# An LSTM cell update as one 24-number scan on VectorE, in place of two dependent instructions

## The chip, the cores and the metric

The kernel runs on one core of a Trainium2 chip, in one launch. The metric is the device time of that launch in microseconds (us); lower is better. TensorE (PE) multiplies matrices, ScalarE (ACT) applies functions, VectorE (DVE) does elementwise work, GpSimd (POOL) fills constants here, SyncE (SP) issues transfers. Each engine takes its instructions in order; engines tell one another by semaphores that something is done.

## The reference

The input x is 4 sequences of 256 steps of 128 numbers. A conditioned attention block and a causal attention give `x + attention`; then an LSTM runs over the 256 steps, a feed-forward block is applied to its outputs, and the result is added to x. Cut to the part that the change touches:

```python
def step(carry, xw_t):                       # 256 times, each on the one before
    prev_h, prev_c = carry                   # 4 x 128
    a = xw_t + prev_h @ Wh                   # 4 x 512
    i = sigmoid(a[:, :H]);       f = sigmoid(a[:, H:2*H])
    o = sigmoid(a[:, 2*H:3*H]);  g = tanh(a[:, 3*H:])
    next_c = f * prev_c + i * g
    next_h = o * tanh(next_c)
    return (next_h, next_c), next_h
x = x + attention(...)
x = x + ffn(lstm(x, h0=cond))                # ffn: gelu(h @ w1 + b1) @ w2 + b2
```

## The kernel before

The program has two stretches. Up to 155 us come the loads, the first block of attention and the feed-forward part that belongs to it. Then a loop over the 256 LSTM steps runs, and everything else that is left (the causal attention in chunks of 32 steps, the second half of the first block, the last feed-forward block) is slipped between the steps.

One step takes four engines in turn. The hidden size of 128 lies on the partitions, so a gate is 128 x 4 numbers (4 sequences), and the four gates are 16 numbers per partition.

- PE (L1738) adds the product with the last h to the gates in the accumulator: 12 small matmuls, four with `wha`, four with `whb`, four with the low part of h. The first eight wait for the high part of h, the last four for its low part.
- ACT (L809) takes the tanh of all 16 numbers into `gates`. Sigmoids are had from tanh, sigmoid(z) = (1 + tanh(z/2)) / 2; the halves are folded into the weights. The gates lie in the order o, i, f, g, and behind them, in the same tile, the old cell (doubled).
- DVE (L1355) forms `pr`, one product for i and g and one for f and the old cell, in one instruction on 8 numbers; then (L1356) the factor from o; then (L1358), which waits for `pr`, adds the two products to the new cell.
- ACT (L811) takes the tanh of the new cell into `h_fac`.
- DVE (L1362) multiplies it with the factor from o: the high part of h, in f16, which PE waits for. L1364, a scan over 12 numbers per partition, leaves what f16 lost as the low part.

The order of all other work is written out by hand. `PLAN` says for each chunk of the attention at which step each of its pieces stands, and `attend(c, t)` issues them on each engine. `VEC_GAP`, `VEC_REST`, `ACT_REST` and `PE_REST` say how many pieces of the first block's second half stand in a step; on DVE a piece of `VEC_GAP` stands between the cell and the wait for its tanh, `attend` and `VEC_REST` stand behind L1364. `INPUTS_AT` and `FFN_STEPS` place the next chunk's gate inputs and the last feed-forward block. An instruction that waits holds up all that stands behind it on its engine.

Before the loop, GpSimd makes `whb` (L552) and fills two constant columns of the tile for h (L555, L556), which the tile names `vaug` in the trace.

Of the kernel before, what the change touches and what calls it, by code (L numbers as in the profile page):

```python
# [23 lines left out]
ALU = mybir.AluOpType  # L24
# [10 lines left out]
P = 128  # L35
# [53 lines left out]
H_SCALE = 4096.0  # L89
W_SCALE = 16.0  # L90
A_SCALE = H_SCALE * W_SCALE
BF16_PARTS = 3
BIAS_ROWS = BF16_PARTS * 4
VW = HD + 1
# [2 lines left out]
def adaln_attention_lstm_ffn(nc, x, cond, w_q, b_q, w_k, b_k, w_v, b_v, w_o, b_o, w_f1, b_f1, w_f2, b_f2,  # L97
                             w_ada, b_ada, W_dq, W_uq, W_dkv, W_uk, W_uv, W_o, Wx, Wh, b_g, w1, b1, w2, b2, out):
    with ExitStack() as ctx:
        def sb(name, shape, dt=F32):  # L100
            return ctx.enter_context(nc.sbuf_tensor(name, shape, dt))
# [4 lines left out]
        def sem(name):  # L106
            return ctx.enter_context(nc.semaphore(name))
# [94 lines left out]
        mo = sb("mo", [P, H, HD])  # L202
        bg_parts = p_mla[0:1].rearrange("p a n -> p (a n)").bitcast(BF16)[:, 0:BIAS_ROWS * D].rearrange("p (r n) -> p r n", n=D)

        gates = sb("gates", [P, 2, 5 * B])
        pr = sb("pr", [P, 2, 2 * B])
        h_fac = sb("h_fac", [P, 2, B, 3])
        h0 = sb("h0", [P, B])
        h_parts = vaug[:].rearrange("p t h v -> p (t h v)").bitcast(F16)[:, 0:2 * S * B * 3].rearrange("p (a t b s) -> p a t b s", a=2, t=S, b=B)
# [108 lines left out]
        w1_ready = sem("w1_ready")  # L318
        gates_mm = sem("gates_mm")
        gates_act = sem("gates_act")  # L320
        c_new = sem("c_new")
        th_act = sem("th_act")
        p_ready = sem("p_ready")
        ff_mm = sem("ff_mm")
        gel_ready = sem("gel_ready")
        y_mm = sem("y_mm")
# [127 lines left out]
        @block.sync  # L454
        def _(sp):
            sp.dma_start(cond4[:], cond).then_inc(ld_ada, 16)
            sp.dma_start(ada_w[:], w_ada).then_inc(ld_ada, 16)
            sp.dma_start(wqkv[:, 0, :], w_q).then_inc(ld_qkv, 16)
            sp.dma_start(wqkv[:, 1, :], w_k).then_inc(ld_qkv, 16)
            sp.dma_start(wqkv[:, 2, :], w_v).then_inc(ld_qkv, 16)  # L460
            sp.dma_start(bqkv[:, 0, :], spread(b_q)).then_inc(ld_qkv, 16)
            sp.dma_start(bqkv[:, 1, :], spread(b_k)).then_inc(ld_qkv, 16)
            sp.dma_start(bqkv[:, 2, :], spread(b_v)).then_inc(ld_qkv, 16)

            sp.dma_start(wd[:, 0, :], W_dq).then_inc(ld_mla, 16)
            sp.dma_start(wd[:, 1, :], W_dkv).then_inc(ld_mla, 16)
            sp.dma_start(wu[0:32, 0, :], W_uq).then_inc(ld_mla, 16)
            sp.dma_start(wu[32:64, 0, :], W_uk).then_inc(ld_mla, 16)
            sp.dma_start(wu[32:64, 1, :], W_uv).then_inc(ld_mla, 16)
            sp.dma_start(wo_m[:], W_o).then_inc(ld_mla, 16)  # L470


            for w_s, w_d, ld in ((wx, Wx, ld_wx), (wh, Wh, ld_rnn)):
                src = w_d.rearrange("k (g n) -> k g n", g=4)
                sp.dma_start(w_s[:, 0, :], src[:, 2, :]).then_inc(ld, 16)
                sp.dma_start(w_s[:, 1:3, :], src[:, 0:2, :]).then_inc(ld, 16)
                sp.dma_start(w_s[:, 3, :], src[:, 3, :]).then_inc(ld, 16)
                if ld is ld_wx:
                    for bb in range(B):
                        sp.dma_start(x_tb[bb:P:B, :, :], x_steps[bb]).then_inc(ld_xtb, 16)  # L480
                    bsrc = row(b_g).rearrange("a (g n) -> a g n", g=4)
                    sp.dma_start(bg[:, 0, :], bsrc[:, 2, :]).then_inc(ld_wx, 16)
                    sp.dma_start(bg[:, 1:3, :], bsrc[:, 0:2, :]).then_inc(ld_wx, 16)
                    sp.dma_start(bg[:, 3, :], bsrc[:, 3, :]).then_inc(ld_wx, 16)
            sp.dma_start(wo_c[:], w_o).then_inc(ld_cff, 16)
            sp.dma_start(bo_c[:], spread(b_o)).then_inc(ld_cff, 16)
            sp.dma_start(wf1[:], w_f1).then_inc(ld_cff, 16)
            sp.dma_start(bf1[:], column(b_f1, FC), allow_slow_non_contiguous=True).then_inc(ld_cff, 16)
            sp.dma_start(wf2[:], w_f2.rearrange("(c p) d -> p c d", p=P)).then_inc(ld_cff, 16)
            sp.dma_start(bf2[:], spread(b_f2)).then_inc(ld_cff, 16)  # L490
            sp.dma_start(w1s[:], w1).then_inc(ld_rnn, 16)
            sp.dma_start(b1s[:], column(b1, FC), allow_slow_non_contiguous=True).then_inc(ld_rnn, 16)
            sp.dma_start(w2s[:], w2.rearrange("(c p) d -> p c d", p=P)).then_inc(ld_rnn, 16)
            sp.dma_start(b2s[:], row(b2)).then_inc(ld_rnn, 16)

            sp.wait_ge(adaR_ready, 1)
            sp.dma_start(bf1_rows, spread(b_f1)).then_inc(ld_bf1, 16)
            sp.wait_ge(bias_part, 2 * BF16_PARTS - 1)
            sp.dma_start(bg_rows[:], bg_parts).then_inc(bias_ready, 16)

            for p, (c, a, z) in enumerate(PIECES):
                sp.wait_ge(y_ready, p + 1)
                sp.dma_start(out_steps[c, a // B:z // B], o_sb[a:z, c % 2, :]).then_inc(stored[c % 2], 16)
            for k in range(2):
                sp.wait_ge(stored[k], 16 * sum(c % 2 == k for c, _, _ in PIECES))

        @block.gpsimd
        def _(pool):
# [29 lines left out]
                                        pattern=[[0, STEPS], [-1, 4], [0, B]], channel_multiplier=1).then_inc(masks, 1)  # L538
                pool.wait_ge(masks, 13 + i)

            pool.wait_ge(w_ready, 4)
            bias = bg[:].rearrange("a g n -> a (g n)")
            for i in range(BF16_PARTS):
                part = bg_parts[:, 4 * i:4 * i + 4, :].rearrange("a g n -> a (g n)")
# [3 lines left out]
                    nc.gpsimd.tensor_tensor(bias, bias, part, ALU.subtract).then_inc(bias_part, 1)  # L548
                    pool.wait_ge(bias_part, 2 * i + 2)

            pool.wait_ge(w_ready, 7)
            nc.gpsimd.tensor_tensor(whb[:], wh[:], wha[:], ALU.subtract).then_inc(w_ready, 1)  # L552

            pool.wait_ge(pv_mm, len(UNITS) // 2)
            nc.gpsimd.memset(h_off[:, :, :, 0], -1.0).then_inc(h_consts, 1)  # L555
            nc.gpsimd.memset(h_off[:, :, :, 1], 0.0).then_inc(h_consts, 1)  # L556
            pool.wait_ge(w1_ready, 1)
# [5 lines left out]
        def _(act):  # L563
# [44 lines left out]
            act.wait_ge(w_mla_mm, 1)  # L608
            nc.scalar.activation(w_mla[:, 0, :], bank[:, 4, 0:D], ACT.Copy).then_inc(w_mla_ready, 1)
            nc.scalar.activation(w_mla[:, 1:3, :].rearrange("p a n -> p (a n)"), bank[:, 5, D:3 * D], ACT.Copy).then_inc(w_mla_ready, 1)  # L610
            act.wait_ge(ld_wx, 16 * 6)
            for w in (wx, bg):
                for g0, g1, f in ((0, 3, .5), (3, 4, 1.)):
                    nc.scalar.mul(w[:, g0:g1, :], w[:, g0:g1, :], A_SCALE * f).then_inc(w_ready, 1)

            nc.scalar.preload_act_table_set(TANH_EXP)
# [117 lines left out]
            o_copy(3)  # L734
            until(first, "up")
            until(first, "third")
            act.wait_ge(ld_rnn, 16 * 7)
            for g0, g1, f in ((0, 3, .5), (3, 4, 1.)):
                nc.scalar.mul(wh[:, g0:g1, :], wh[:, g0:g1, :], W_SCALE * f).then_inc(w_ready, 1)
            act.wait_ge(w_ready, 6)  # L740
            nc.scalar.activation(flat(wha[:]), flat(wh[:]), ACT.Copy).then_inc(w_ready, 1)
            nc.scalar.mul(h0[:], condT[:], H_SCALE).then_inc(w_ready, 1)
            until(first, "fourth")
# [58 lines left out]
            for t in range(S):  # L802
                k = t % 2
                src = bank[:, 6 + (t // STEPS) % 2, (t % STEPS) * GW:(t % STEPS + 1) * GW]

                if t == 0:
                    act.wait_ge(c_new, 1)
                act.wait_ge(gates_mm, t + 1)
                nc.scalar.activation(gates[:, k, 0:GW], src, ACT.Tanh, scale=1.0 / A_SCALE).then_inc(gates_act, 1)  # L809
                act.wait_ge(c_new, t + 2)  # L810
                nc.scalar.activation(h_fac[:, k, :, 1], gates[:, 1 - k, 4 * B:5 * B], ACT.Tanh, scale=0.5).then_inc(th_act, 1)  # L811
                for c in attending(t):
                    attend(c, t)
                go_on(second, ACT_REST, t)
                for p, i in feeding(t):
                    if i in (2, 3):
                        gelu(p, range(2 * i - 4, 2 * i - 2))
# [3 lines left out]
        def _(vec):  # L821
# [11 lines left out]
            def step(ins, signal=None):  # L833
                done(go(ins, signal))
# [492 lines left out]
                    done(mr_ready)  # L1327
                    V.tensor_tensor(mo[:], tr[:, :, 0:HD], rdm[:].unsqueeze(2).to_broadcast([P, H, HD]), ALU.mult).then_inc(mo_normed, 1)

            step(V.memset(gates[:], 0.0), c_new)  # L1330
            vec.wait_ge(h_consts, 2)
            attend(0, PLAN[0]["vb"][0])
            for q in range(2):
# [17 lines left out]

            for t in range(S):
                k = t % 2
                vec.wait_ge(gates_act, t + 1)
                V.scalar_tensor_tensor(pr[:, k, :], gates[:, k, B:3 * B], 1.0, gates[:, k, 3 * B:5 * B], ALU.add, ALU.mult).then_inc(p_ready, 1)  # L1355
                V.tensor_scalar(h_fac[:, k, :, 2], gates[:, k, 0:B], 1.0, 0.5 * H_SCALE, ALU.add, ALU.mult)  # L1356
                vec.wait_ge(p_ready, t + 1)
                V.scalar_tensor_tensor(gates[:, 1 - k, 4 * B:5 * B], pr[:, k, B:2 * B], 0.5, pr[:, k, 0:B], ALU.mult, ALU.add).then_inc(c_new, 1)  # L1358
                go_on(second, VEC_GAP, t)

                vec.wait_ge(th_act, t + 1)
                V.tensor_tensor(h_off[:, t, :, 2], h_fac[:, k, :, 2], h_fac[:, k, :, 1], ALU.mult).then_inc(h_ready, 1)  # L1362
                vec.wait_ge(h_ready, t + 1)
# [1 line left out]
                                     h_off[:, t].rearrange("p b s -> p (b s)"), 0.0, ALU.mult, ALU.subtract).then_inc(hb_ready, 1)  # L1365
                for c in attending(t):
                    attend(c, t)
                go_on(second, VEC_REST, t)
                for p, i in feeding(t):
                    if i == 6:  # L1370
# [4 lines left out]
        def _(pe):  # L1375
# [34 lines left out]
            for k in range(2):  # L1410
                for t in range(4):
                    ins = T.transpose(bank[:, k, t * P:(t + 1) * P], x_tb[:, 4 * k + t, :], ident[:])
                ins.then_inc(x_turned, 1)
            pe.wait_ge(w_ready, 2)
            pe.wait_ge(woT_ready, 1)
            T.matmul(bank[:, 6, :], woT[:], wx[:].rearrange("p g n -> p (g n)"), start=True, stop=True).then_inc(wox_mm, 1)

# [261 lines left out]
            pe.wait_ge(masks, 15)  # L1679
            inputs_of(0, range(0, 5))  # L1680
            pe.wait_ge(vbd_ones, 1)
            pe.wait_ge(w_ready, 9)
            for g in range(4):
                T.matmul(bank[:, 6, g * B:(g + 1) * B], wh[:, g, :], h0[:], start=False, stop=True, skip_group_check=True)

# [99 lines left out]
```

## Time and profile before

| | |
|---|---|
| time, median of 3 runs | 580.17 us (579.87 to 582.31) |
| profiled execution: span from first to last instruction | 578.5 us; about 1.7 us of the run's time lie around it |
| busy: PE, PE weight loads, DVE, ACT, POOL | 412.2, 311.5, 370.7, 241.9, 25.8 us |
| loop of 256 steps, first to last gate tanh | 155.3 to 571.7 us |
| TensorE clock granted in the loop | about half of full speed |

The profile is of one execution. Times in rows are us from the start of the span, unless a column says ns. Of a busy share one cannot read what a stage waits for; the chain of work that ended last, and the rows of one step, show it.

### The profile page before, as it was taken

The page shows a single profiled execution, that of the slowest core. Times are in us where ns is not written, and L with a number is a line of the kernel's source. Part 1 is how long each engine was busy: PE and PEld are TensorE (multiplying, and loading weights), DVE is VectorE, ACT ScalarE, POOL GpSimd, SP SyncE. Part 2 cuts the span into 40 slices and gives each one's busy share as a digit, 9 for nine tenths or more (in the row PEclk, how much of TensorE's full clock was granted, in tenths as well). Part 3 has the DMA queues.
Part 4 walks back from the last instruction along what each step waited for, and adds up shares of the span by engine and source line. Part 5 has one row for each costly group of instructions (what it writes and reads, how often), then busy time and mean ns, then how long its engine had stood idle before and what let it go on. Part 6 is the DMA issues. An engine that isn't in the chain of part 4 may idle for free.

```text
span 578.5 us, 15950 instructions
## 1 busy us (share of the span) xinstructions
PE 412.2 (71%) x6273; PEld 311.5 (54%) x6273; DVE 370.7 (64%) x1967; ACT 241.9 (42%) x937; POOL 25.8 (4%) x35
## 2 busy tenths in 40 slices
PE   3464866676776798995478686886885675787876
PEld 2234644455555575874356554654653564575654
DVE  7888448369687776567756656666667664444443
ACT  1267966363435345234334424334424334333332
POOL 8012000003100000000000000000000000000000
PEclk9676987595555555575555555555555555555555
DMA  7400000000000000000000000000000000000000
GB/s 190 116 0 1 4 2 1 1 1 1 1 2 3 2 3 1 2 2 2 2 3 2 3 1 1 3 2 2 2 3 1 3 2 2 6 11 6 6 11 6
DMA packets 8966, 5.95 MB, mean 10 GB/s; under 512 B 2004, under 2 KB 8252, under 8 KB 8892
## 3 DMA queue, kind: packets, MB, share of 16 engines
q1 hardware_dynamic: 7708, 4.03, 2.8%
q8 instruction: 49, 0.80, 0.6%
q10 hardware_dynamic: 1184, 0.92, 0.5%
q14 instruction: 25, 0.20, 0.1%
HBM read 4.42 MB, written 0.52 MB: 9 GB/s over the span
## 4 chain that ended last, share of the span: by engine, by line
PE 37%; DVE 36%; ACT 18%; issue 7%; DMA 1%; ACTq 0%; DVEq 0%
PE bank L1738 17%; ACT h_fac L811 7%; DVE vaug L1362 6%; ACT gates L809 6%; DVE pr L1355 6%; DVE gates L1358 5%; PE bank L1563 4%; DVE h_fac L1356 3%; PE bank L1640 2%; PE bank L1465 2%; DVE mx L1293 1%; ACT p_mla L756 1%; PE bank L1538 1%; PE bank L1530 1%; PE bank L1512 1%
## 5 line engine op out<-in xcount | busy, mean ns | idle before, releaser
L1738 PE MATMUL bank<-vaug,wha 128*128 128x4 f16 x2040 | 123.8, 169 | 100.0 <-DVE vaug L1362 94.8
L1738 PEld LDWEIGHTS bank<-vaug,wha 128*128 128x128 f16 x2040 | 96.4, 106 | 162.1 <-DVE vaug L1362 160.0
L809 ACT ACTIVATE gates<-bank 128x16 f32<-128x16 f32 x256 | 47.2, 184 | 146.5 <-PE bank L1738 144.6
L811 ACT ACTIVATE h_fac<-gates 128x4 f32<-128x4 f32 x256 | 53.1, 207 | 110.7 <-DVE gates L1358 110.7
L1355 DVE SCALAR_TENSOR_TENSOR pr<-gates 128x8 f32<-128x8 f32 x256 | 42.7, 167 | 77.8 <-ACT gates L809 73.6
L1362 DVE TENSOR_TENSOR vaug<-h_fac 128x4 f16<-128x4 f32 x256 | 43.3, 169 | 67.8 <-ACT h_fac L811 67.6
L1738 PE MATMUL bank<-vaug,whb 128*128 128x4 f16 x1020 | 62.7, 166 | 0.0
L1364 DVE TENSOR_TENSOR_SCAN vaug<-h_fac,vaug 128x12 f16<-128x12 f32 x256 | 46.7, 183 | 8.7
L1563 PE MATMUL bank<-kT,qz 32*128 32x32 f32 (+7 forms) x256 | 50.1, 520 | 0.8 <-ACT kT L775 0.4
L1738 PEld LDWEIGHTS bank<-vaug,whb 128*128 128x128 f16 x1020 | 46.7, 103 | 0.0
L1356 DVE TENSOR_SCALAR h_fac<-gates 128x4 f32<-128x4 f32 x256 | 41.5, 162 | 0.0
L1358 DVE SCALAR_TENSOR_TENSOR gates<-pr 128x4 f32<-128x4 f32 x256 | 41.5, 162 | 0.0
L756 ACT ACTIVATE p_mla<-bank,mx 128x32 f32<-128x32 f32 (+7 forms) x128 | 39.6, 374 | 1.9 <-DVE mx L1293 1.8
L1303 DVE STREAM_TRANSPOSE pt_mla<-p_mla 128x192 f32<-128x192 f32 (+5 forms) x96 | 32.8, 356 | 1.3 <-PE bank L1585 0.6
L1563 PEld LDWEIGHTS bank<-kT,qz 32*128 32x128 f32 x256 | 29.4, 305 | 2.6 <-ACT kT L775 0.8
L1585 PE MATMUL bank<-vbd,pt_mla 128*32 128x36 f32 x1152 | 27.8, 257 | 2.9 <-DVE pt_mla L1303 1.2
L1293 DVE TENSOR_REDUCE mx<-bank 128x2 f32<-128x320 f32 (+7 forms) x48 | 25.6, 539 | 1.9 <-PE bank L1568 1.9
L1585 PEld LDWEIGHTS bank<-vbd,pt_mla 128*32 128x32 f32 x1152 | 21.0, 157 | 5.3 <-DVE pt_mla L1303 4.3
L1444 PE MATMUL bank<-qS,kS 32*128 32x128 f16 x256 | 11.4, 237 | 15.4 <-ACT q_sq L636 7.7
L1636 PE MATMUL bank<-x_tm,wx 128*128 128x128 f32 x64 | 21.5, 472 | 0.0
L1727 PE MATMUL bank<-w2s,ta 128*128 128x128 f32 (+2 forms) x72 | 21.0, 451 | 0.4 <-ACT ta L799 0.4
L1444 PEld LDWEIGHTS bank<-qS,kS 32*128 32x128 f16 x256 | 6.6, 100 | 20.8 <-ACT q_sq L636 9.9
(292 smaller groups left out, 680.4 us busy)
## 6 DMA issues: line engine op xcount, KB each, us to landing
x_tm<-in_x ACTq DMA_DIRECT2D x1, 512.0 KB, 5.3
x_tb<-in_x SPq DMA_DIRECT2D x4, 128.0 KB, 2.7
wf<-in_L_cond_w_f SPq DMA_DIRECT2D x2, 256.0 KB, 3.4
out_y<-tb SPq DMA_DIRECT2D x7, 64.0 KB, 2.0
ada_w<-in_L_cond_w_ada SPq DMA_DIRECT2D x1, 384.0 KB
ada_b<-in_L_cond_b_ada ACTq DMA_DIRECT2D x1, 384.0 KB, 5.8
w1s<-in_L_ffn_w SPq DMA_DIRECT2D x1, 256.0 KB
w2s<-in_L_ffn_w SPq DMA_DIRECT2D x1, 256.0 KB
```

The lines of the kernel that those rows point to most:

```text
L756: ins = nc.scalar.activation(p_mla[:, m % 2, i * n:(i + 1) * n], bank[:, at, i * n:(i + 1) * n], ACT.Exp, bias=mx[:, m % 2, i:i + 1])
L809: nc.scalar.activation(gates[:, k, 0:GW], src, ACT.Tanh, scale=1.0 / A_SCALE).then_inc(gates_act, 1)
L811: nc.scalar.activation(h_fac[:, k, :, 1], gates[:, 1 - k, 4 * B:5 * B], ACT.Tanh, scale=0.5).then_inc(th_act, 1)
L1303: V.transpose(pt_mla[:, to, n * part:n * (part + 1)], p_mla[:, m % 2, n * part:n * (part + 1)]).then_inc(mt_ready, 1)
L1355: V.scalar_tensor_tensor(pr[:, k, :], gates[:, k, B:3 * B], 1.0, gates[:, k, 3 * B:5 * B], ALU.add, ALU.mult).then_inc(p_ready, 1)
L1356: V.tensor_scalar(h_fac[:, k, :, 2], gates[:, k, 0:B], 1.0, 0.5 * H_SCALE, ALU.add, ALU.mult)
L1358: V.scalar_tensor_tensor(gates[:, 1 - k, 4 * B:5 * B], pr[:, k, B:2 * B], 0.5, pr[:, k, 0:B], ALU.mult, ALU.add).then_inc(c_new, 1)
L1362: V.tensor_tensor(h_off[:, t, :, 2], h_fac[:, k, :, 2], h_fac[:, k, :, 1], ALU.mult).then_inc(h_ready, 1)
L1364: V.tensor_tensor_scan(h_low[:, t].rearrange("p b s -> p (b s)"), h_fac[:, k].rearrange("p b s -> p (b s)"), h_off[:, t].rearrange("p b s ...
L1563: T.matmul(bank[:, at, i * n:(i + 1) * n], qz[rows, c % 2, bs[i]].rearrange("p j t -> p (j t)"), kT[rows, bs[i], 0:n], start=(i == 0), sto ...
L1585: ins = T.matmul(bank[32 * b:32 * b + 32, 5, g * GROUP * VW:(g + 1) * GROUP * VW], pt_mla[:, place, i * n + kb * STEPS:i * n + (kb + 1) * ...
L1738: ins = T.matmul(acc[:, g * B:(g + 1) * B], w[:, g, :], h, start=False, stop=True, skip_group_check=True)
```

## The change

The cell update becomes one `tensor_tensor_scan` (op: state = in0 x state + in1) over 6 numbers for each of the 4 sequences, 24 per partition. With s a fixed scale, t_i and t_f the tanh values of the halved gates, g the tanh of the fourth, and c the old cell times s, the six states of one sequence are: s; t_i s + s; that times g; that divided by c, plus t_f; half of that plus a half; that times c. The last is s times the new cell. The quotient needs 1/c, which a new `reciprocal` makes after each step, and a c that is never zero, which a new bitwise or on the cell's bits sees to (it sets one bit of the exponent, which every cell above 2^-63 has set anyway).

So the gates move: ACT writes them to strided places among the scan's two inputs and into a third piece. `wx`, `wh` and the bias are kept in the order f, g, i, o, loaded with two transfers each in place of three and scaled by three instructions in place of two. Constants of the scan's inputs are filled by seven new memsets on GpSimd. The tiles reuse older ones: `hn` holds the scan's inputs (and o), `small` the scan's output.

```diff
-        gates = sb("gates", [P, 2, 5 * B])
-        pr = sb("pr", [P, 2, 2 * B])
+        gates = hn[:].rearrange("p a t h -> p (a t h)")[:, 0:6 * B * CW].rearrange("p (k a b s) -> p k a b s", k=2, a=3, b=B)
+        cell_out = small[:, 0:2 * CW * B // TILES, :].rearrange("p k t -> p (k t)").rearrange("p (k b s) -> p k b s", k=2, b=B)
+        cell_in1, cell_in0, gate_o = gates[:, :, 0], gates[:, :, 1], gates[:, :, 2, :, 0]
+        gates_out = [bass.AP(hn, 3 * k * B * CW + 3, [[3 * TILES * H, P], [(B - 1) * CW + 4, 2], [B * CW - 1, 2], [CW, B]]) for k in range(2)]
...
             pool.wait_ge(pv_mm, len(UNITS) // 2)
+            nc.gpsimd.memset(cell_in1[:, :, :, 0:2], C_SCALE).then_inc(cell_consts, 1)
+            nc.gpsimd.memset(cell_in1[:, :, :, 2:6:3], 0.0).then_inc(cell_consts, 1)
...
             nc.gpsimd.memset(h_off[:, :, :, 0], -1.0).then_inc(h_consts, 1)
...
-                nc.scalar.activation(gates[:, k, 0:GW], src, ACT.Tanh, scale=1.0 / A_SCALE).then_inc(gates_act, 1)
-                act.wait_ge(c_new, t + 2)
-                nc.scalar.activation(h_fac[:, k, :, 1], gates[:, 1 - k, 4 * B:5 * B], ACT.Tanh, scale=0.5).then_inc(th_act, 1)
+                nc.scalar.activation(gates_out[k], src.rearrange("p (u v b) -> p u v b", u=2, v=2), ACT.Tanh, scale=1.0 / A_SCALE).then_inc(gates_act, 1)
+                act.wait_ge(c_new, t + 1)
+                nc.scalar.activation(h_fac[:, k, :, 1], cell_out[:, k, :, 5], ACT.Tanh, scale=1.0 / C_SCALE).then_inc(th_act, 1)
...
                 k = t % 2
+                if t:
+                    vec.wait_ge(c_inverse, t)
                 vec.wait_ge(gates_act, t + 1)
-                V.scalar_tensor_tensor(pr[:, k, :], gates[:, k, B:3 * B], 1.0, gates[:, k, 3 * B:5 * B], ALU.add, ALU.mult).then_inc(p_ready, 1)
-                V.tensor_scalar(h_fac[:, k, :, 2], gates[:, k, 0:B], 1.0, 0.5 * H_SCALE, ALU.add, ALU.mult)
-                vec.wait_ge(p_ready, t + 1)
-                V.scalar_tensor_tensor(gates[:, 1 - k, 4 * B:5 * B], pr[:, k, B:2 * B], 0.5, pr[:, k, 0:B], ALU.mult, ALU.add).then_inc(c_new, 1)
+                V.tensor_tensor_scan(cell_out[:, k].rearrange("p b s -> p (b s)"), cell_in0[:, k].rearrange("p b s -> p (b s)"),
+                                     cell_in1[:, k].rearrange("p b s -> p (b s)"), 0.0, ALU.mult, ALU.add).then_inc(c_new, 1)
+                V.tensor_scalar(h_fac[:, k, :, 2], gate_o[:, k], 1.0, 0.5 * H_SCALE, ALU.add, ALU.mult).then_inc(o_ready, 1)
                 go_on(second, VEC_GAP, t)
+                if t < S - 1:
+                    vec.wait_ge(c_new, t + 1)
+                    V.tensor_scalar(cell_in0[:, 1 - k, :, 5].bitcast(I32), cell_out[:, k, :, 5].bitcast(I32), C_LEAST_BITS, None,
+                                    ALU.bitwise_or).then_inc(c_kept, 1)
+                vec.wait_ge(o_ready, t + 1)
                 vec.wait_ge(th_act, t + 1)
                 V.tensor_tensor(h_off[:, t, :, 2], h_fac[:, k, :, 2], h_fac[:, k, :, 1], ALU.mult).then_inc(h_ready, 1)
...
                 for c in attending(t):
                     attend(c, t)
+                if t < S - 1:
+                    vec.wait_ge(c_kept, t + 1)
+                    V.reciprocal(cell_in0[:, 1 - k, :, 3], cell_in0[:, 1 - k, :, 5]).then_inc(c_inverse, 1)
                 go_on(second, VEC_REST, t)
```

On DVE, a step of the loop in which a row maximum of the attention (`mx`) stands is before, from one gate instruction to the next (the list names a scan SCALAR_TENSOR_TENSOR, and the tile of h `vaug`):

```order
L1355 SCALAR_TENSOR_TENSOR pr<-gates 128x8 [waits gates_act]
L1356 TENSOR_SCALAR h_fac<-gates 128x4
L1358 SCALAR_TENSOR_TENSOR gates<-pr 128x4 [waits p_ready]
L1362 TENSOR_TENSOR vaug<-h_fac 128x4 [waits th_act]
L1364 SCALAR_TENSOR_TENSOR vaug<-h_fac,vaug 128x12 [waits h_ready]
L1293 TENSOR_REDUCE mx<-bank 128x2 [waits mp_ready,ms_mm]
```

The same step in the changed kernel, whose lines are numbered 10 to 24 higher, has the scan into `small`, and the or and the reciprocal on pieces of `hn`:

```order
L1369 SCALAR_TENSOR_TENSOR small<-hn 128x24 [waits gates_act,c_inverse]
L1371 TENSOR_SCALAR h_fac<-hn 128x4
L1375 TENSOR_SCALAR hn<-small 128x4 [waits c_new]
L1380 TENSOR_TENSOR vaug<-h_fac 128x4 [waits th_act,o_ready]
L1382 SCALAR_TENSOR_TENSOR vaug<-h_fac,vaug 128x12 [waits h_ready]
L1305 TENSOR_REDUCE mx<-bank 128x2 [waits mp_ready,ms_mm]
L1388 RECIPROCAL hn<-hn 128x4 [waits c_kept]
```

Two instructions ahead of the cell's tanh became one, the or stands between the cell and the wait for its tanh, and the reciprocal stands behind the attention's piece and ahead of the next step's scan, which now waits for it too.

On GpSimd, the end of the stretch before the loop, from the last piece of the bias on, is before:

```order
L545 CAST p_mla<-bg 1x512 [waits bias_part]
L552 TENSOR_TENSOR whb<-wh,wha 128x512 [waits w_ready,bias_part]
L555 MEMSET vaug 128x1024 [waits pv_mm]
L556 MEMSET vaug 128x1024
L558 CAST ada_w<-w1s 128x512 [waits w1_ready]
```

And in the changed kernel:

```order
L552 CAST p_mla<-bg 1x512 [waits bias_part]
L559 TENSOR_TENSOR whb<-wh,wha 128x512 [waits w_ready,bias_part]
L562 MEMSET hn 128x2x4x2 [waits pv_mm]
L563 MEMSET hn 128x2x8
L564 MEMSET hn 128x2x4
L565 MEMSET hn 128x2x4
L566 MEMSET hn 128x2x4
L567 MEMSET hn 128x4
L568 MEMSET hn 128x4
L569 MEMSET vaug 128x1024
L570 MEMSET vaug 128x1024
L572 CAST ada_w<-w1s 128x512 [waits w1_ready]
```

The seven small memsets stand ahead of the two long ones.

## Rows read from the trace of the kernel before

**Rows 1.** The chain that ended last, within the loop, shares by line.

```profile
by line: PE bank L1738 23.6%; ACT h_fac L811 10.2%; DVE vaug L1362 8.4%; ACT gates L809 7.9%; DVE pr L1355 7.8%; issue 7.5%; DVE gates L1358 6.3%; PE bank L1563 5.3%; DVE h_fac L1356 3.9%; PE bank L1640 2.5%; DVE mx L1293 1.8%; PE bank L153
```

**Rows 2.** Timeline of one step: start us, us, instruction [idle before <-releaser].

```profile
544.21 0.18 ACT L809 ACTIVATE gates<-bank 128x16 f32<-128x16 f32 x1 [0.78 <-PE bank L1738]
544.42 0.17 DVE L1355 SCALAR_TENSOR_TENSOR pr<-gates 128x8 f32<-128x8 f32 x1 [0.58 <-ACT gates L809]
544.51 0.16 DVE L1356 TENSOR_SCALAR h_fac<-gates 128x4 f32<-128x4 f32 x1
544.62 0.16 DVE L1358 SCALAR_TENSOR_TENSOR gates<-pr 128x4 f32<-128x4 f32 x1
544.82 0.21 ACT L811 ACTIVATE h_fac<-gates 128x4 f32<-128x4 f32 x1 [0.43 <-DVE gates L1358]
...
545.06 0.17 DVE L1362 TENSOR_TENSOR vaug<-h_fac 128x4 f16<-128x4 f32 x1 [0.27 <-ACT h_fac L811]
545.26 0.18 DVE L1364 TENSOR_TENSOR_SCAN vaug<-h_fac,vaug 128x12 f16<-128x12 f32 x1
...
545.28 0.27 PE L1738 MATMUL bank<-vaug,wha 128*128 128x4 f16 x4 [1.11 <-DVE vaug L1362]
...
545.81 0.18 ACT L809 ACTIVATE gates<-bank 128x16 f32<-128x16 f32 x1 [0.27 <-PE bank L1738]
```

**Rows 3.** DVE instructions in the loop by form: busy us, mean ns | idle before.

```profile
L1364 DVE TENSOR_TENSOR_SCAN vaug<-h_fac,vaug 128x12 f16<-128x12 f32 x256 | 46.7, 183 | 8.7
L1362 DVE TENSOR_TENSOR vaug<-h_fac 128x4 f16<-128x4 f32 x256 | 43.3, 169 | 67.8 <-ACT h_fac L811 67.6
...
L1358 DVE SCALAR_TENSOR_TENSOR gates<-pr 128x4 f32<-128x4 f32 x256 | 41.5, 162 | 0.0
...
L1000 DVE TENSOR_SCALAR sm<-sm 128x4 int32<-128x4 int32 x4 | 0.6, 155 | 0.0
...
L1084 DVE RECIPROCAL sm<-sm 128x4 f32<-128x4 f32 x2 | 0.4, 177 | 0.1
```

**Rows 4.** ACT instructions in the loop, same columns.

```profile
L764 ACT ACTIVATE coT<-bank 128x128 f32<-128x128 f32 x7 | 2.6, 376 | 0.0
L775 ACT ACTIVATE kT<-bank 128x128 f32<-128x128 f32 x7 | 1.9, 276 | 0.0
```

**Rows 5.** Who DVE waited for in the loop: us in total, times, longest us.

```profile
DVE pr L1355 <- ACT gates L809: 73.6, 171, 1.6
```

**Rows 6.** Timeline of DVE: two steps with a piece of the attention.

```profile
442.42 0.43 DVE L1303 STREAM_TRANSPOSE pt_mla<-p_mla 128x256 f32<-128x256 f32 x1
443.08 0.17 DVE L1355 SCALAR_TENSOR_TENSOR pr<-gates 128x8 f32<-128x8 f32 x1 [0.23 <-ACT gates L809]
...
447.24 0.67 DVE L1293 TENSOR_REDUCE mx<-bank 128x2 f32<-128x512 f32 x1
...
447.90 0.17 DVE L1355 SCALAR_TENSOR_TENSOR pr<-gates 128x8 f32<-128x8 f32 x1
```

**Rows 7.** Timeline: first and last step in which PE came late.

```profile
177.49 0.17 DVE L1362 TENSOR_TENSOR vaug<-h_fac 128x4 f16<-128x4 f32 x1 [0.20 <-ACT h_fac L811]
...
177.78 0.27 PE L1738 MATMUL bank<-vaug,wha 128*128 128x4 f16 x4
...
566.16 0.17 DVE L1362 TENSOR_TENSOR vaug<-h_fac 128x4 f16<-128x4 f32 x1 [0.27 <-ACT h_fac L811]
...
566.40 0.29 PE L1738 MATMUL bank<-vaug,wha 128*128 128x4 f16 x4
```

**Rows 8.** Timeline of DVE before the loop, one instruction.

```profile
131.13 4.15 DVE L1053 TENSOR_SCALAR sm<-sm 128x4 f32<-128x4 f32 x1
```

**Rows 9.** Timeline of POOL: two short memsets, and the last before the loop.

```profile
0.27 0.10 POOL L1775 MEMSET const-float32-1.0<- 128x1 f32 x1
0.31 0.10 POOL L1775 MEMSET const-bfloat16-1.0<- 128x1 bf16 x1
...
133.40 1.85 POOL L556 MEMSET vaug<- 128x1024 f16 x1
```

## What I predict

> **What bounds the kernel now.** I read the chain of work that ended last first, cut to the loop. Its largest shares are the links of one LSTM step in turn: the 12 matmuls, the two tanhs of ACT, and DVE's three instructions for the cell and one for h [rows 1]. No engine is full there; the loop is bound by a ring of dependent instructions. The second view is the timeline of one step near the end, where nothing is in the way [rows 2]. From one gate tanh (544.21) to the next (545.81) are 1.60 us: 0.21 to `pr`, 0.20 to the cell, 0.20 to its tanh, 0.24 to h, 0.22 to the first matmul, 0.53 to the next gates. The second instruction behind the gates, the factor from o, begins beside `pr`, so the cell's 0.20 is the 0.167 of `pr` and a semaphore of 0.03. Third I read the waits of DVE: in 171 of 256 steps `pr` waits for the gates, in the other 85 the attention's or the first block's pieces fill DVE up to its start, to within some 0.1 us [rows 5]. The same question on PE goes to the timeline: h to first matmul is 0.22 where PE waits; in 33 steps it is more, the first with 0.29 and the last with 0.24 [rows 7]. In those PE's side work sets the step.
>
> **The change, part by part.**
>
> *The cell.* From `pr` to the tanh of the cell are 0.40 us [rows 2]. The change puts one scan of 24 numbers there, and 0.035 from its end to the tanh, as now from the cell's end (544.62 + 0.16 to 544.82). No scan of 24 is in the trace. The scan of 12 takes 183 ns; instructions on 4 numbers take 162, or 169 with the same f16 output [rows 3]. So each further number costs 1.75 to 2.6 ns, and 24 take 204 to 214. The bounds are 183 (nothing more for more numbers) and 214; I take 210, between the two slopes. The link becomes 0.245, and a step that only the ring binds is 0.155 shorter.
>
> The Trainium skill (DVE: opcode table, instruction layouts, handler registers and perf-mode slots, section Datapath and trigger behaviour) says that the built-in scan feeds its result back to an earlier stage and so runs at half throughput. With the engine's clock of 0.96 GHz from the Trainium skill (VectorE: DVE Perf Modes, Specifications) an estimate by that rule is 2.1 ns a number and 208 ns for 24; a full-rate scan would be 196, and the sum 3.6 us lower. The slopes of this trace lie about the half-rate figure.
>
> *The gates' tanh.* ACT writes the 16 results to 16 strided places, before in one run. The nearest rows are two copies of 128 numbers from the accumulator: 376 ns into strided places, 276 into runs of 32 [rows 4], so 0.8 ns a number, 13 ns for 16. The bounds are 0 and, if all of the first row's time were its writing (376 / 128 = 2.9 a number), 47; I take 13, the difference of the two rows. A step of the ring is then 0.142 shorter, times 256: 36.4 us.
>
> *The or.* An integer instruction of this size takes 155 ns [rows 3]. It can begin when the scan has ended, 0.245 behind the scan's start, and ends at 0.40; h can start at 0.245 + 0.24 = 0.485. The wait for the cell's tanh covers it. A piece of `VEC_GAP` stands ahead of it in 25 steps; with a small one the or ends at 0.46, still covered. I cost it at nothing; without that cover it would be 25 x 0.1 = 2.5 us.
>
> *The reciprocal.* It takes 177 ns [rows 3]. A DVE instruction begins about 0.08 before the end of the one ahead when it waits for nothing, so the reciprocal ends 0.10 behind the end of the step's last piece of side work, and with a semaphore of 0.035 the next scan may start 0.13 behind it. Bounds are 0.05 (a hidden tail) and 0.21 (no overlap at all). The stretch from h to the next gate instruction is as long as before, 0.22 + 0.53 + 0.21 = 0.96, so what was idle there before is what the reciprocal has. Two steps show it: after the transpose 0.23 us were idle, enough; after the row maximum (447.24 + 0.67 = 447.91) `pr` began at 447.90 with none [rows 6]. Counted over the timeline of the loop: 39 steps had under 0.03 us (I take 0), 46 had 0.03 to 0.13 (0.08), 35 up to 0.25 (0.19), 50 up to 0.35 (0.30), 86 more. The first two make up the 85 steps above. At 0.13 they lose 39 x 0.13 + 46 x 0.05 = 7.4 us. What is queued behind the scan's new wait is the ring itself, so all of it counts.
>
> *PE.* Its side work per step stays and the step gets shorter. In the 33 steps where PE already came late nothing of the 0.142 arrives: 33 x 0.142 = 4.7 us off. In some 14 more it becomes late by a few hundredths; I leave that in the range.
>
> *Before the loop.* Seven memsets of 8 to 32 numbers are put ahead of the two long ones on GpSimd. A small DVE instruction there takes 4.15 us, from 131.13 to 135.28, and ends when the second long memset does, at 133.40 + 1.85 = 135.25 [rows 8, 9]; it lies on the chain. Short memsets start 0.04 apart and take 0.10 [rows 9], so seven add 0.3 to 0.7 us to that stall: +0.4.
>
> On this the Trainium skill (SBUF — State Buffer, section SBUF: two separate sides) says that VectorE and GpSimd share a pair of ports as an exclusive lock, which blocks the loser for the whole instruction. The stalled row is what that would look like. If only the two long memsets held the lock, the 0.4 would not arrive.
>
> *Weights, loads, order of gates.* Two transfers for three and three small multiplies for two end tens of microseconds ahead of their use or cost a tenth; nothing.
>
> **Sum.** 36.4 - 7.4 - 4.7 - 0.4 = 23.9 us. The profiled span becomes 578.5 - 23.9 = 554.6; with the 1.7 around it, that is the median of 580.17 less 23.9, 556.3. I say 556.
>
> **Rivals.**
>
> *The reciprocal is dearer in the filled steps.* For it: 85 steps have no room, and two semaphores stand ahead of one instruction. At 0.21 the loss is 39 x 0.21 + 46 x 0.13 + 35 x 0.02 = 14.9 in place of 7.4: 564. Against it: side instructions overlap their neighbours all through the loop.
>
> *More of the hop arrives.* A strided write that costs nothing and a reciprocal at 0.05 give 256 x 0.155 - 39 x 0.05 - 33 x 0.155 - 0.4 = 32.2: 548. A scan of 183 on top would save another 6 us.
>
> *The long scan is slow, so that the change does not do what it says.* If its price per number were not that of the 12-number scan and it took 300 ns, 256 x 0.052 - 7.4 - 1.7 - 0.4 = 3.8 are left: 576. Against it: nothing in the rows of scans.
>
> *Slower: the reciprocal decides the steps.* It stands behind the attention's piece on an engine that takes its work in order. If the way from the last piece to the scan's start were 0.40, the idle counts above give 39 x 0.40 + 46 x 0.32 + 35 x 0.21 + 50 x 0.10 = 42.7; with 2 for PE and 0.4 before the loop that is more than the 36.4: 589. The turn is at 0.35, where the loss is 39 x 0.35 + 46 x 0.27 + 35 x 0.16 + 50 x 0.05 = 34.2. Against it: an instruction of 177 ns would have to hold the engine for twice its time.
>
> **How the numbers follow.** The forecast has a chance of 0.63, the dearer reciprocal 0.14, more of the hop 0.15, the slow scan 0.05, the slower case 0.03. About 0.5%, 3 us, is what a measurement of this kernel can tell from no change. Faster by more than that: the first three and two fifths of the slow scan, 0.94; within it 0.03; slower 0.03. The forecast's own range is 549 to 563. The range for 8 in 10 takes in the first two rivals and, above them, a strided write towards its upper bound (another 256 x 0.02 = 5 us), and below them part of the shorter scan: 546 to 568.
>
> **What would show it.** A free step near the end at about 1.46 us, with 0.21 for the scan of 24 and 0.245 from its start to the tanh; gates to scan at 0.23, not 0.21. The or wholly inside the wait for the tanh. In steps with a row maximum, the scan released by the reciprocal and not by the gates, 0.13 behind the maximum's end; in the last 55 steps never. More steps than 33 in which PE comes late. It would be wrong if the free step stayed above 1.50, if scans waited for the reciprocal in many more than 85 steps, or if new waits came up among the attention's pieces, which now have fewer microseconds from step to step.

## The result, and the profile after

The changed kernel took 583.72 us (median of 6 runs, 580.79 to 586.55), the kernel before 580.92 (6 runs, 579.87 to 582.31): a ratio of 1.005, 95% interval 1.0029 to 1.0071. I had predicted 556 and a range from 546 to 568. The forecast was wrong: 24 us of gain did not come.

The profile is of the shortest of the 6 runs, with a span of 578.9 us. In it the loop begins at 152.75 us, before at 155.28. From 60 to 116 us that run was granted a mean TensorE clock of 0.82, the one of before 0.76. Two of the experiments below, both with the change, show the same pair: at 0.76 the loop begins at 154.74, at 0.82 at 152.48. So most of the earlier start goes with the clock and not with the change. I compare the loops: 416.5 us before, 419.4 after, 3 us longer.

The DVE instructions in the loop by form, from 155 us on (busy us, mean ns | idle before), answer to [rows 3]:

```profile
L1369 DVE TENSOR_TENSOR_SCAN small<-hn 128x24 f32<-128x24 f32 x254 | 52.7, 207 | 79.2 <-ACT hn L821 73.6
...
L1375 DVE TENSOR_SCALAR hn<-small 128x4 int32<-128x4 int32 x253 | 43.2, 171 | 0.2 <-DVE small L1369 0.2
L1388 DVE RECIPROCAL hn<-hn 128x4 f32<-128x4 f32 x254 | 40.0, 157 | 0.0
```

Each instruction is within 20 ns of its forecast: the long scan takes 207 ns (210 was put in), the reciprocal 157 (177), the or 171 (155). One free step in the timeline, to set beside [rows 2]:

```profile
549.22 0.20 ACT L821 ACTIVATE hn<-bank 128x16 f32<-128x16 f32 x1 [0.85 <-PE bank L1759]
549.52 0.21 DVE L1369 TENSOR_TENSOR_SCAN small<-hn 128x24 f32<-128x24 f32 x1 [0.58 <-ACT hn L821]
...
549.76 0.21 ACT L823 ACTIVATE h_fac<-small 128x4 f32<-128x4 f32 x1 [0.34 <-DVE small L1369]
549.76 0.17 DVE L1375 TENSOR_SCALAR hn<-small 128x4 int32<-128x4 int32 x1
550.07 0.17 DVE L1380 TENSOR_TENSOR vaug<-h_fac 128x4 f16<-128x4 f32 x1
```

The gates end at 549.42 and the scan starts at 549.52; the tanh ends at 549.97 and h starts at 550.07. Both gaps are 0.10 us, also in the median of all steps; before they were 0.03. DVE was idle in both. What filled them shows in the chain of waits of the same step (start us, us, what; a q behind an engine's name is its queue):

```profile
549.22 0.21 ACT hn L821
549.43 0.03 issue
549.46 0.02 DVEq L1368
549.48 0.04 issue
549.52 0.22 DVE small L1369
549.74 0.02 issue
549.76 0.22 ACT h_fac L823
549.98 0.03 issue
550.01 0.02 DVEq L1379
550.03 0.04 issue
550.07 0.18 DVE vaug L1380
```

L1368 is the wait for the gates, L1379 the wait for the tanh. The change gave the scan a second wait (for the reciprocal) and h a second (for the factor from o). Of the two waits ahead of one instruction, one becomes an instruction of the queue here, and it is the one written last, both times the one that comes late. In the chain of before no such piece of DVE stands anywhere in the loop.

Summed over the steps, from the starts of the instructions in each trace (before, after, and two of the experiments below), us:

| link | before | after | both pairs swapped | and reciprocal early |
|---|---|---|---|---|
| gates to first cell instruction | 56.3 | 79.6 | 66.8 | 60.1 |
| that to the cell's tanh | 101.5 | 61.7 | 61.7 | 61.8 |
| tanh to h | 61.4 | 81.1 | 63.0 | 62.8 |
| h to first matmul | 63.9 | 63.5 | 68.5 | 70.6 |
| first matmul to next gates | 134.2 | 134.4 | 134.5 | 134.6 |
| loop, first to last gates | 416.5 | 419.4 | 393.9 | 389.2 |

So the hop that was to go is gone (39.8 us less), and two other links took 43.0 more.

### The profile page after: what moved, and what is told of

The parts are those of the page before. It is cut to its first block, busy times and chain, and to the rows that moved or that the text cites. A ratio compares the mean times of both kernels' runs of the same rounds, so it can differ in the third digit from the quotient of the medians.

```text
span 578.9 us, 16720 instructions
## 1 busy us (share of the span) xinstructions
PE 407.7 (70%) x6273; PEld 308.2 (53%) x6273; DVE 402.1 (69%) x2220; ACT 247.0 (43%) x940; POOL 28.1 (5%) x42
## 4 chain that ended last, share of the span: by engine, by line
PE 35%; DVE 34%; ACT 18%; issue 11%; DVEq 1%; DMA 1%; ACTq 0%
PE bank L1759 16%; DVE small L1369 8%; ACT h_fac L823 8%; DVE vaug L1380 6%; ACT hn L821 6%; PE bank L1584 4%; DVE mx L1305 2%; PE bank L1661 2%; PE bank L1486 1%; PE bank L1559 1%; PE bank L1551 1%; DVE vaug L1382 1%; PE bank L1450 1%; ACT q_sq L650 1%; DMA x_tm<-in_x 1%
## 5 line engine op out<-in xcount | busy, mean ns | idle before, releaser
L821 ACT ACTIVATE hn<-bank 128x16 f32<-128x16 f32 x256 | 51.0, 199 | 165.1 <-PE bank L1759 164.0
L1369 DVE TENSOR_TENSOR_SCAN small<-hn 128x24 f32<-128x24 f32 x256 | 53.1, 207 | 79.6 <-ACT hn L821 74.0
L823 ACT ACTIVATE h_fac<-small 128x4 f32<-128x4 f32 x256 | 53.7, 210 | 90.2 <-DVE small L1369 90.2
L1375 DVE TENSOR_SCALAR hn<-small 128x4 int32<-128x4 int32 x255 | 43.5, 171 | 0.2 <-DVE small L1369 0.2
L1388 DVE RECIPROCAL hn<-hn 128x4 f32<-128x4 f32 x255 | 40.1, 157 | 0.0
L1371 DVE TENSOR_SCALAR h_fac<-hn 128x4 f32<-128x4 f32 x256 | 36.9, 144 | 0.2 <-issue 0.2
```

The costliest lines, as they stand in the source:

```text
L821: nc.scalar.activation(gates_out[k], src.rearrange("p (u v b) -> p u v b", u=2, v=2), ACT.Tanh, scale=1.0 / A_SCALE).then_inc(gates_act, 1)
L823: nc.scalar.activation(h_fac[:, k, :, 1], cell_out[:, k, :, 5], ACT.Tanh, scale=1.0 / C_SCALE).then_inc(th_act, 1)
L1369: V.tensor_tensor_scan(cell_out[:, k].rearrange("p b s -> p (b s)"), cell_in0[:, k].rearrange("p b s -> p (b s)"), cell_in1[:, k].rearrang ...
L1375: V.tensor_scalar(cell_in0[:, 1 - k, :, 5].bitcast(I32), cell_out[:, k, :, 5].bitcast(I32), C_LEAST_BITS, None, ALU.bitwise_or).then_inc(c ...
L1388: V.reciprocal(cell_in0[:, 1 - k, :, 3], cell_in0[:, 1 - k, :, 5]).then_inc(c_inverse, 1)
```

## The experiments

Theory W: of two waits, the one written last is an instruction of its own, and costs about 0.065 us when it is the one that ends last. Rival R: DVE's added instructions and its longer queue hold scan and h up.

**Both pairs of waits in the other order.** No work changes.

```diff
-                if t:
-                    vec.wait_ge(c_inverse, t)
                 vec.wait_ge(gates_act, t + 1)
+                if t:
+                    vec.wait_ge(c_inverse, t)
...
-                vec.wait_ge(o_ready, t + 1)
                 vec.wait_ge(th_act, t + 1)
+                vec.wait_ge(o_ready, t + 1)
```

> The changed kernel with the two pairs of waits on VectorE in the other order: scan waits for the gates first and then for the reciprocal, h for the tanh first and then for the factor of o. No work changes. Theory W (a second wait is an instruction of its own that holds the wait written last, and VectorE starts the real instruction about 0.065 us after it): gates to scan falls from 0.301 to about 0.235, tanh to h from 0.312 to about 0.24, a free step from 1.60 to 1.46 us, the loop from 419 to 394 to 398 us, the time to 558 to 562. Rival R (the or, the reciprocal and the longer queue on VectorE themselves hold up scan and h): the links stay at 0.30 and 0.31 and the time within 3 us of the changed kernel's 583.

It took 557.26 us, just under the range expected, a ratio to before of 0.9595 (0.9564 to 0.9626); a second measurement gave 557.46 and 0.9598 (0.957 to 0.9627). The chain of a free step has no queue instruction any more:

```profile
520.26 0.22 ACT h_fac L823
520.48 0.02 issue
520.51 0.18 DVE vaug L1380
520.69 0.04 issue
520.73 0.50 PE bank L1759 x12
521.23 0.02 issue
521.26 0.21 ACT hn L821
521.47 0.02 issue
521.49 0.22 DVE small L1369
```

In the median a step is 1.47 us long, from gates to scan are 0.233, from tanh to h 0.243. R falls: the or, the reciprocal and the longer queue are all still there.

**Only the scan's pair swapped.** The edit is the first half of the one above.

> Only the pair of waits ahead of the 24-number scan in the other order; h keeps its pair. Theory W: gates to scan 0.235, tanh to h stays at 0.312, free step 1.535, loop about 405, time about 569. Rival R: 583, as the changed kernel. If only one of the two links were due to the waits, this run and the one with both swapped tell which.

It took 572.57 us, 0.987 (0.9836 to 0.9904), 3.6 us above what I expected. In the median gates to scan are 0.233, tanh to h 0.312 as in the changed kernel, a step 1.535: each link answers to its own pair. The loop got 9.2 us shorter than that of the changed kernel, and not 256 x 0.068 = 17.4: what the scans are late by, beyond the median, grew from 2.7 to 7.9 us, and what PE is late by grew by 3.0.

**The kernel before, with two waits each.** Here no work is added at all.

```diff
+                vec.wait_ge(c_new, t + 1)
                 vec.wait_ge(gates_act, t + 1)
                 V.scalar_tensor_tensor(pr[:, k, :], ...
...
+                vec.wait_ge(c_new, t + 2)
                 vec.wait_ge(th_act, t + 1)
                 V.tensor_tensor(h_off[:, t, :, 2], ...
```

> The kernel before, with a second wait, long fulfilled (the cell's own semaphore), written ahead of the waits of pr for the gates and of h for the tanh. Nothing else. Theory W: both links grow by 0.065 to 0.075, a free step from 1.60 to about 1.735, and less what the steps with a late PE absorb, the time grows by 27 to 34 us, to 608 to 615. Rival R: no change, 581, since no work was added.

It took 614.25 us, 1.0586 (1.055 to 1.0621). Two waits that were already fulfilled cost 34 us. The chain shows the same queue instructions, now in the old ring:

```profile
575.34 0.19 ACT gates L809
575.53 0.03 issue
575.56 0.02 DVEq L1355
575.58 0.04 issue
575.62 0.17 DVE pr L1356
...
576.02 0.22 ACT h_fac L811
576.24 0.03 issue
576.26 0.02 DVEq L1363
576.28 0.04 issue
576.33 0.18 DVE vaug L1364
```

Both links grew by 0.070 us in the median (0.217 to 0.287 and 0.240 to 0.310).

**The same two waits, written behind the late ones.**

```diff
                 vec.wait_ge(gates_act, t + 1)
+                vec.wait_ge(c_new, t + 1)
...
                 vec.wait_ge(th_act, t + 1)
+                vec.wait_ge(c_new, t + 2)
```

> The kernel before with the same two added waits as in the run before (each long fulfilled), but written behind the wait for the gates and the wait for the tanh. Theory W says that only the wait written last becomes an instruction of its own; here that is the fulfilled one, which is passed while VectorE idles, so the links stay at 0.217 and 0.240 and the time at 581, within 2 us of the kernel before. Rival (any second wait costs, whichever is late): as with the waits in the other order, about 614.

It took 582.06 us, 1.0026 (1.0012 to 1.004): 1.2 us more than before between the medians, 2.3 at the upper end of the interval. The links stand at 0.216 and 0.240 again, and the loop takes 417.2 us, 0.8 more than before. It is not the number of waits that costs 34 us but which of them is written last. What the remaining 1.2 us are is open.

**Both pairs swapped, and the reciprocal between h and its low part.** The swaps are those above; the rest of the edit:

```diff
+                if t < S - 1:
+                    vec.wait_ge(c_kept, t + 1)
+                    V.reciprocal(cell_in0[:, 1 - k, :, 3], cell_in0[:, 1 - k, :, 5]).then_inc(c_inverse, 1)
                 vec.wait_ge(h_ready, t + 1)
                 V.tensor_tensor_scan(h_low[:, t]...
...
                 for c in attending(t):
                     attend(c, t)
-                if t < S - 1:
-                    vec.wait_ge(c_kept, t + 1)
-                    V.reciprocal(cell_in0[:, 1 - k, :, 3], cell_in0[:, 1 - k, :, 5]).then_inc(c_inverse, 1)
```

> Both pairs swapped, and the reciprocal moved from behind the attention's piece to between h and the 12-number scan for its low part. Theory: steps whose VectorE is filled no longer wait for the reciprocal, which by the prediction's count is worth some 7 us (85 steps): 551 to 555, against 558 to 562 with both swapped alone; late scans fall to under 10. Rival: the reciprocal holds up the low part of h, which PE's last four matmuls wait for, so gates to matmul grows by up to 0.1 us a step: 565 to 580.

It took 552.77 us, 0.953 (0.9503 to 0.9557): faster than both kernels, and than the swap alone, from whose interval it is clear. A step with a row maximum on DVE, first with the swap alone, then with the reciprocal early:

```profile
439.27 0.67 DVE L1305 TENSOR_REDUCE mx<-bank 128x2 f32<-128x512 f32 x1
439.86 0.17 DVE L1388 RECIPROCAL hn<-hn 128x4 f32<-128x4 f32 x1
440.13 0.21 DVE L1369 TENSOR_TENSOR_SCAN small<-hn 128x24 f32<-128x24 f32 x1
```

```profile
434.35 0.17 DVE L1383 RECIPROCAL hn<-hn 128x4 f32<-128x4 f32 x1
434.48 0.18 DVE L1385 TENSOR_TENSOR_SCAN vaug<-h_fac,vaug 128x12 f16<-128x12 f32 x1
434.58 0.67 DVE L1305 TENSOR_REDUCE mx<-bank 128x2 f32<-128x512 f32 x1
435.26 0.21 DVE L1369 TENSOR_TENSOR_SCAN small<-hn 128x24 f32<-128x24 f32 x1
```

From the start of the maximum to that of the scan are 0.86 us in the first, 0.68 in the second. Late scans (over 0.02 behind the median) go from 68 to 4, and the time of all scans beyond the median from 7.3 us to 1.0. The low part of h starts 0.20 behind h in the median of both, and the link from the first matmul to the gates stands (134.6 us against 134.5), so the rival's price did not come.

**The gates in one run.** On top of both swaps ACT writes its 16 numbers contiguously, and memsets fill the places that are left empty; the scan then works on constants, so the recurrence is not computed. The edit on ACT:

```diff
-  nc.scalar.activation(gates_out[k], src.rearrange("p (u v b) -> p u v b", u=2, v=2), ACT.Tanh, ...
+  nc.scalar.activation(hn[:].rearrange("p a t h -> p (a t h)")[:, (3 * k + 2) * B * CW:(3 * k + 2) * B * CW + GW], src, ACT.Tanh, ...
```

> Both pairs swapped, and ACT writes the 16 gates in one run instead of to strided places; the scan then runs on constants, so the recurrence is not computed. By the prediction's 13 ns a step for the strided write (199 ns now against 184 before in the profiles, 15 ns): the gates' tanh back at 184 ns, the time 3 to 4 us under the kernel with both pairs swapped. Rival (the 15 ns do not lie on the ring): equal times.

It took 556.45 us, 0.9581 (0.9556 to 0.9606), against 557.46 with the strided write, where 3 to 4 us less were expected: the intervals overlap, so the time tells nothing. The rows do. The gates' tanh, with the strided write and in one run:

```profile
L821 ACT ACTIVATE hn<-bank x256: 182/200/215, 154.7 to 548.6; 128x16 f32<-128x16 f32 x128
```

```profile
L822 ACT ACTIVATE hn<-bank x256: 165/183/200, 156.9 to 548.6; 128x16 f32<-128x16 f32 x128
```

The median is 17 ns shorter. Against the second measurement of the strided write, gates to scan fall from 0.231 to 0.216, so the tanh does lie on the ring, and the loop from 394.0 to 391.7 us. That is less than 256 x 0.015 = 3.8, since late scans and PE take more (1.0 and 0.7 us). The profiled run of the one-run kernel began its loop 1.9 us later, which hides most of the 2.3 in its time.

## Why the prediction was wrong, point by point

- **The cell's hop.** Put at 0.155 us a step; measured 0.397 less 0.241, 0.156. Right. The scan takes 207 ns; from 12 to 24 numbers each costs 2.0 ns. By the rule of the Trainium skill (DVE: opcode table, instruction layouts, handler registers and perf-mode slots, Datapath and trigger behaviour) the estimate was 208. The trace, at 207, agrees with half rate.
- **The gates' tanh.** Put at 13 ns for the strided write; 199 after against 184 before is 15, and in one run 17 less. Right.
- **The or.** Covered, as said: with the waits swapped, tanh to h is 0.243 against 0.240.
- **The step that failed** is the price of the two links that got a second wait. The prediction took each at its old price: "gates to scan at 0.23", and "h can start at 0.245 + 0.24 = 0.485". I asked what stands queued behind a new wait and when its condition comes true, but not what the wait itself costs as an instruction, and so put that at nothing. It is 0.07 us at each of two places in the ring, 0.14 a step: nearly the whole of the 0.142 that I counted as gain. Gates to scan measured 0.301, tanh to h 0.312 where 0.24 was put, and a step stayed at 1.60 in the median, above the 1.50 that was to show the forecast wrong.
- **It could be read.** The rows of the changed order showed both waits on one instruction, and the chain of before has the price just ahead of the loop, where the attention's transpose, with two waits, was on it. Between the end of PE's work and the transpose lie three pieces, 0.10 us in all; L1326, which has no such piece, follows the same PE line after 0.03 (151.01 to 151.04):

```profile
149.39 0.38 PE bank L1585 x8
149.77 0.03 issue
149.80 0.02 DVEq L1302
149.82 0.05 issue
149.87 0.06 DVE pt_mla L1303
```

- **The reciprocal in filled steps.** Put at 7.4 us: 85 steps, and in the fullest the scan 0.13 behind the last piece. In the changed kernel that distance came true. In this step the maximum ends at 466.16, the reciprocal at 466.25, and the scan starts at 466.29:

```profile
465.49 0.67 DVE L1305 TENSOR_REDUCE mx<-bank 128x2 f32<-128x512 f32 x1
466.08 0.17 DVE L1388 RECIPROCAL hn<-hn 128x4 f32<-128x4 f32 x1
466.29 0.21 DVE L1369 TENSOR_TENSOR_SCAN small<-hn 128x24 f32<-128x24 f32 x1
```

But the lengthened ring hid most of the cost (24 late scans, 2.7 us). With the pairs swapped, the wait written last is the one for the reciprocal, and where that one ends last the price of the wait moves there: in the step shown above (439.27) the reciprocal ends at 440.03 and the scan starts at 440.13, 0.19 behind the maximum, with this piece in the chain:

```profile
440.07 0.02 DVEq L1368
```

In 49 of the 68 late steps the scan starts 0.10 behind the reciprocal's end; in the changed kernel it is 0.034 in the 18 steps where the reciprocal ends last. So the cost with the swap, 7.3 less the 0.9 of before, is near 7.4 in part by luck: fewer steps were late than counted, and those behind a maximum paid 0.19 and not 0.13. The early place takes the cost away.

- **PE.** Put at 4.7 us. With the swap PE's lateness grows from 6.5 us in 33 steps to 11.2 in 47: 4.7. Right; with the early reciprocal it is 13.2 in 54, which is why only some 4.7 of the 6.3 us won there arrive in the loop.
- **Before the loop.** Put at 0.4 us: the stalled DVE instruction takes 4.50 us, against 4.15 in [rows 8]. Right in size; the seven short memsets put the first long one off by 0.27 (from 128.94 to 129.21). The row, from the timeline of the changed kernel, also fits what the Trainium skill (SBUF — State Buffer, SBUF: two separate sides) says of a loser that is blocked for the other's whole instruction. Here it is held for a whole row of them, up to 132.74, and the last long memset ends at 132.72:

```profile
128.24 4.50 DVE L1065 TENSOR_SCALAR sm<-sm 128x4 f32<-128x4 f32 x1
```

With the waits in the other order the terms of the cell, the gates' tanh and PE hold, that of the reciprocal comes near in part by luck, and the kernel takes 557.3 and 557.5 us, where 556 was predicted. None of the rivals was this one. The dearer reciprocal came nearest: it named the two semaphores ahead of one instruction, but charged them in the filled steps alone and left the links of the ring at their old price. The slower case asked for 0.35 us from the last piece to the scan, and that is 0.13 in the changed kernel.

## What to carry to other kernels

When a change gives an instruction a second wait, price the wait itself: the chain of waits names it by the queue of the engine. Write the wait that ends last first and the ones long fulfilled behind it; here the order of two pairs of lines was worth 26 us of 584. Where now the one, now the other ends last, the price moves with the order, as it did to the reciprocal. Then look for a place for new side work in a gap between two dependent instructions, ahead of the long pieces and not behind them; here that was worth another 4.5 us. The runs show all this for DVE in one kernel.

## What the runs showed of the hardware that I had not expected

Ahead of one DVE instruction with two waits, the wait written last is, in these runs, an instruction of its own of 21 ns. If it is the one that ends last, the real instruction starts 0.10 us behind the end of the work it waits for, and not 0.03. If it was fulfilled while the engine idled, it costs nothing that the links show (0.216 and 0.240 against 0.217 and 0.240).
